# A graph and transformer kernel on one core: GpSimd waits for each set of gathered rows before it fetches the next

## The reference

```
xn = _layernorm(x, axis=-1)
h_fwd = xn @ W_forward.T
h_rev = xn @ W_reverse.T
messages = h_fwd[src] * direction[:, 0:1] + h_rev[src] * direction[:, 1:2]
scores = leaky_relu(einsum('ef,hf->eh', messages, attn_forward[0]), 0.2)
...
outs = [segment_sum(messages * norm[:, hd:hd + 1], dst) for hd in range(4)]
x = x + gnn(xn, ...) + mix(xn[None], ...)[0]
x = x + ffn(_layernorm(x)[None], ...)[0]
```

## Time and profile before

| | us |
|---|---|
| median of 3 runs | 2891.04 |
| lowest and highest run | 2889.53, 2899.61 |
| span of the profiled execution (the profile gives no other time for it) | 2911.8 |
| GpSimd busy in it | 1185.6 |
| VectorE busy in it | 1693.7 |
| TensorE busy in it | 2563.1 |
| the 400 gathers of the mixing stage, busy | 412.8 |

### The profile page before, as it was taken

The page is one execution under the profiler, slowest core; times in us unless marked ns, Lnnn a source line. Parts: engine busy times, 40 slices in busy tenths (PEclk is TensorE's granted clock), DMA queues, the critical chain, the costliest instruction groups (busy, mean ns, idle before and its releaser), DMA issues. The chain is left out here.

```text
span 2911.8 us, 47805 instructions
## 1 busy us (share of the span) xinstructions
PE 2563.1 (88%) x16831; PEld 2377.1 (82%) x16831; DVE 1693.7 (58%) x4350; ACT 1330.1 (46%) x2855; POOL 1185.6 (41%) x1326
## 2 busy tenths in 40 slices
PE   6788899899989998998995999549899999998998
PEld 6778898889888988885675888439898888898898
DVE  4566777677766776555666232355556444444665
ACT  3234565455545554445532122212245454444687
POOL 1223453345434543456840222366654455554100
PEclk9889999999999999998985899856889899999899
DMA  4211112111211120124214444332221232233011
GB/s 106 66 37 37 37 44 66 37 37 43 68 37 37 42 68 23 47 55 107 83 54 118 151 143 139 117 108 84 86 87 38 71 97 84 86 95 92 21 45 29
DMA packets 137166, 205.25 MB, mean 70 GB/s; under 512 B 35134, under 2 KB 98430, under 8 KB 136803
## 3 DMA queue, kind: packets, MB, share of 16 engines
q1 hardware_dynamic: 99842, 107.97, 12.4%
q0 software_dynamic: 37088, 94.23, 11.8%
HBM read 168.50 MB, written 33.62 MB: 69 GB/s over the span
## 5 line engine op out<-in xcount | busy, mean ns | idle before, releaser
L922 POOL DMA_INDIRECT gat<-table,srcT x400 | 412.8, 1032 | 359.0 <-DVE m L2640 259.4
L1066 POOL DMA_INDIRECT x_rows<-table,srcT x392 | 381.6, 974 | 306.4 <-PE pg L1834 146.7
L588 PE MATMUL pa<-w,act 128*125 128x256 f32 x2400 | 362.3, 289 | 12.4 <-DVE act L2399 11.9
L588 PE MATMUL pb<-hT,w 128*128 128x378 f32 (+1 forms) x1920 | 342.3, 315 | 10.9 <-ACT gf L1905 8.5
L588 PEld LDWEIGHTS pa<-w,act 128*125 128x125 f32 x2400 | 317.5, 189 | 17.3 <-DVE act L2399 16.5
L2154 ACT ACTIVATE gf<-pb,bne 128x378 f32<-128x378 f32 (+1 forms) x320 | 194.2, 607 | 252.7 <-PE pb L588 137.5
L588 PEld LDWEIGHTS pb<-hT,w 128*128 128x128 f32 x1920 | 291.7, 192 | 14.9 <-ACT gf L1905 6.4
L1905 ACT ACTIVATE gf<-pb,b1s 128x378 f32<-128x378 f32 (+1 forms) x320 | 165.9, 519 | 139.7 <-PE pb L588 93.8
L2399 DVE TENSOR_TENSOR act<-gf,act 128x378 fp32r<-128x378 f32 (+1 forms) x320 | 153.7, 483 | 102.6 <-ACT act L1908 66.1
L588 PE MATMUL pb<-act,fw 128*128 128x378 f32 (+1 forms) x960 | 169.7, 329 | 29.2 <-ACT gf L2154 28.7
L588 PEld LDWEIGHTS pb<-act,fw 128*128 128x128 f32 x960 | 152.6, 202 | 31.9 <-issue 31.9
(11 more groups left out here) (492 smaller groups left out, 5694.9 us busy)
## 6 DMA issues: line engine op xcount, KB each, us to landing
e<-in_L_ffn_W_dram SPq DMA_DIRECT2D x40, 512.0 KB, 4.6
spill<-m SPq DMA_DIRECT2D x80, 170.0 KB
msg<-spill SPq DMA_DIRECT2D x40, 340.0 KB, 2.9
yslots<-yo SPq DMA_DIRECT2D x64, 128.0 KB, 2.0
fraw<-in_L_ffn_W_dram SPq DMA_DIRECT2D x32, 256.0 KB
w1r<-in_L_mix_W_dram SPq DMA_DIRECT2D x7, 1024.0 KB, 4.9
gat<-table,srcT POOLq DMA_INDIRECT x400
x_rows<-table,srcT POOLq DMA_INDIRECT x392
```

The lines of the kernel that those rows point to most:

```text
L588: mm = nc.tensor.matmul(ps, lhs(l), rhs(r), start=first and n == 0, stop=last and n == 2)
L922: pool.indirect_dma_start(out=gat[:, i % 2, c, :], out_offset=None, in_=table0, in_offset=bass.IndirectOffsetOnAxis(ap=srcT[:, i * GC + c: ...
L1066: pool.indirect_dma_start(out=x_rows[:, n % UB, c, :], out_offset=None, in_=table1, in_offset=bass.IndirectOffsetOnAxis(ap=srcT[:, at:at + ...
```

## The change

From set 1 on, `fetch(i)` also waits until all five gathers of set i - 1 have landed.

```
         def fetch(i):
 
             if i >= 2:
                 pool.wait_ge(s["msg_ready"], i - 1)
+            if i >= 1:
+                pool.wait_ge(s[f"gat{(i - 1) % 2}"], 16 * GC * ((i - 1) // 2 + 1))
             for c in range(GC):
                 pool.indirect_dma_start(out=gat[:, i % 2, c, :], out_offset=None, in_=table0,
                                         in_offset=bass.IndirectOffsetOnAxis(ap=srcT[:, i * GC + c:i * GC + c + 1], axis=0)
                                         ).then_inc(s[f"gat{i % 2}"], 16)
```

## The result

The change made the kernel faster, outside the range: 2856.38 us, median of 4 runs (2853.17 to 2860.18), against 2890.28 (2888.86 to 2899.61, 4 runs) before. The ratio is 0.9874, with a 95% interval of 0.9855 to 0.9893, or 34 us. The forecast had been no change.

What follows compares the result with a forecast made beforehand. It took PE to lead the path, with GpSimd mostly idle. GpSimd would gain 0.8 + 12.6 + 3 = 16.4 us, all hidden, adding 0 to the median 2891.04: 2891 us, range 2884 to 2900.

Steps and rivals of the forecast that it cites:

- Price of a met wait: On GpSimd in the mixing stage: an already met wait costs about 0.01 us, 79 of them 0.8 us, hidden by idle time.
- landing: Mixing stage: L, from a set's last gather's end until its rows count as landed, taken as 2.2 us (1.8 to 2.7).
- How often: Mixing stage: seven sets following closely on the set ahead wait for landing, 12.6 us together (9.8 to 16.1).
- The rows themselves: Mixing stage: rows land 2 us later in seven sets, still before VectorE reads them, so VectorE never waits.
- tail pays a little: Rival: with L between 2.8 and 3.7 us the mixing stage's last message is late; 2891 to 2896 us, chance 0.07.
- Roots: Mixing stage: delays end in GpSimd idle time, no row root moves; rival of late roots: 2906 to 2921 us, chance 0.05.
- moved gathers: Gathers of later-starting sets last 85 ns longer each, 3 us, hidden; rival of slow moved sets: 2898 us, chance 0.02.
- Added to the path: 0: Whole kernel: the 16.4 us added on GpSimd in the mixing stage leaves the execution time unchanged.
- faster: Rival: fewer back-to-back gathers hold VectorE up less; must give 15 us, 2876 us or less; chance 0.04.
- What bounds the kernel now: Whole kernel: the last-ending chain gives PE 34%, POOL 1%; only GpSimd time that another engine waits for counts.
- Every set pays its landing: Rival: GpSimd's queue pace becomes issue plus landing for all sets, 142 to 213 us more, 3033 to 3104 us; chance 0.01.

Runs made afterwards that it cites:

- e12: As e10, plus about two pauses per round of five gather pairs in the last stage; 2857.49 us, 0.9776 of the kernel before.
- e4: The changed kernel, and in the last stages each pair of x_rows gathers also waits until the pair ahead has landed; 3144.4 us, 1.0870 of the kernel before.
- e3: The kernel before, no landing wait, two small GpSimd power operations before sets 1, 12, 31, 50, 69, 73 and 77; 2854.23 us, 0.9867 of before.
- e15: The kernel before with 16 rows per gather in place of 128, leaving out most messages; 2944.62 us, 1.0076 of before.
- e10: The kernel before, no landing wait, one GpSimd power operation as a pause before every set but the first; 0.9876 of before.
- e5: The kernel before with 32 bytes fetched per row in place of 544, leaving out the right messages; 2895.28 us, 1.0008 of before.

## Why the prediction was wrong

- *Price of a met wait* and *landing*: right. The unmet waits last L less the gap. After, twelve of the thirteen first gathers that waited started 1.9 to 2.8 us behind the gather ahead, most of them 2.25 to 2.5, against the 2.2 taken. The longest is 3.50 (set 79), above the 2.7 at which the prediction ended L, and inside its hard bound of 3.70.
- *How often*: too small. The sum was 12.6 us in 7, measured are 31.7 us in 13. The last layer comes earlier and its sets lie closer, so nine first gathers wait there. The term stood beside the path, as said.
- *The rows themselves*: VectorE waited for a gather once, 2.8 us at set 79, where the prediction had it never wait. This is the place and the mechanism of the rival *tail pays a little*, and its price of 0 to 4.5 us.
- *Roots* and *moved gathers*: right. ScalarE's waits for the roots are 35.3 and 36.5 us, and the longest gather is 2184 ns, so neither late roots nor slow moved sets came.
- *"Added to the path: 0"*: this step failed. The change took 34 us off the path. The prediction asked whom a later GpSimd would delay, and put at nothing what the row of ten gathers costs as it is. The runs show that cost: updates of PE up to 7.7 us late beside sets 1, 12, 31 and 50, and stretches shorter by 8.3 to 9.2 us each once the rows are broken. The 13.43 us of idle time ahead of the root behind set 12 were read as cover, and 8.2 us of them were the stall itself: VectorE computed the statistics for that root late, because it had stood still. From the start of set 11 to that root it is 26.0 us before and 17.8 after, and the idle time after is 1.57 us.
- *The rival "faster"*, at 0.04, had the right place and was put aside on the wrong row. It looked for a hold in the duration of VectorE's message operations. The hold is in the waits between operations, of which 76 us in 21 have "remote" as releaser in the four rows above. The program runs on one core, so these rows should have been followed.
- Its condition, 15 us, was met by the stretches behind two of the four sets already.
- *What bounds the kernel now* leaned on the chain in the earlier trace rows, and that chain says nothing of the mixing stage. It is followed back only to 1508 us; its first long piece is

```profile
1508.33 25.35 PE pa L1500 x125
```

So neither its 1% for POOL nor its 4% for "another core or an unknown queue" is of the stage of the change. The 4% stayed 4% with the change, and fell to 1% in e12, whose pauses are in the last stage.
- *Every set pays its landing*: not in the mixing stage, as forecast. e4 shows it in the last stage, where GpSimd has no other waits in the same places, and there it cost 8.7%. The rule of the Trainium skill, "DMA: Bandwidth & Descriptors", rules for kernel authors, to issue early and wait late pointed the wrong way for this change: waiting earlier was faster here, 0.9874. e3 doesn't contradict it, though: waiting early for the rows wasn't what gained.

## What to carry to other kernels

Look in the list of waits for those whose releaser is unknown, and lay them beside GpSimd's timeline: on this core such waits were semaphore updates that came late. Ask of a chain from which time on it speaks before it is used for a stage. Don't let GpSimd issue ten indirect gathers in a row while PE hands work to other engines; a power operation of 1.2 us between five and five, on a scratch tile, was enough here and costs GpSimd less than a wait for landing. Shorter rows than five gave nothing that could be told from noise in the mixing stage. Idle time behind a place is only cover if its own cause isn't that place.

## What the runs showed of the hardware

- Beside a row of indirect gathers on GpSimd (0.94 us each, 0.30 between), semaphore updates of PE arrive late: up to 7.7 us beside ten (8.9 in e15) and up to 2.5 beside five in the changed kernel (3.0 in e10). In the mixing stage those of VectorE and ScalarE came in time. In the last stages, beside rows of 20 gathers and more, VectorE's link to its own next instruction is held as well (`z` of line 3182 in e5: 10.7 us in 3 waits, 5.4 at most).
- The last held update comes 7.2 to 7.4 us behind the start of a row of five and 14.4 to 14.7 behind the start of a row of ten (medians), about 1.45 us per gather. Measured from the end of a row of ten, the burst begins 1.0 to 2.0 us later before, and 2.5 to 2.7 in e15, where the row is shorter.
- The stalls depend neither on bytes (32 or 544 a row) nor on rows per gather (16 or 128): `qs` waits 27.1, 26.9 and 28.4 us in 4 (e5, e15, before).
- A gap of 0.84 us between two gathers doesn't release the updates, one of 1.43 us does.
- By which path the updates are held stays open, and so does why some come through in the middle of a row, as at 92.40 and 93.86 us before, 8.7 and 10.2 us behind the start of set 0.
- The issue time of a gather is nearly all fixed: 841 ns for 16 rows, 945 for 128 (medians).
